# Cross attention on 64-row tiles: high and low parts of keys and queries placed under one another by DMA

## The chip, the cores and the metric

The kernel runs on one core of a Trainium2 chip. It is one program with one launch. The metric is the time of the whole execution on the device in microseconds (us); here that is the median of three runs. Below, PE is TensorE (PEld its weight loads), DVE is VectorE, ACT is ScalarE, POOL is GpSimd and SP is SyncE, which here only issues DMAs.

## The reference, cut to what matters

The input is x (32 batches, 112 tokens, 512 wide) and a memory of 375 rows of 256 for each batch. A first layer attends to the memory and gates the result. A second layer has causal self attention with two sets of weights (experts, chosen token by token by a mask), then the cross attention to the memory, then a gated MLP with two experts. The change is inside the cross attention:

```
cq = heads(rms_norm(hidden) @ cq_w, 16, 16)          # 112 x 256 -> 16 heads of 16
ck, cv = split(encoder_outputs @ ckv_w)              # 375 x 256 each, 16 heads of 16
scores = (cq / sqrt(16)) . ck                        # 16 heads, 112 x 375
p = softmax(scores)
hidden = hidden + (p . cv) @ cdense_w                # 256 -> 512
```

All is float32. The kernel reaches the accuracy with the matmul type float32r: a value is split into a high part (rounded to that type) and a low part (the rest), and a product a.b is taken as hi.hi + hi.lo + lo.hi.

## The kernel before, in words

The program runs six stages, a to f, one after another on every engine; each engine has its own written order and they meet through semaphores. Stage e is the cross attention. It goes over the 32 batches as a software pipeline in steps s: in step s TensorE computes the keys, values and turned queries of batch s+1, the scores by row of batch s, the scores by key of batch s-1, and the context and output product of batch s-2. The order is written out by hand in `e_pe` (lines 1694 to 1753), `e_act` (1555 to 1587), `e_dve` (1800 to 1827), `e_sp` (1504 to 1512) and `e_pool`.

One batch goes through these steps:

- `e_key_products` (line 1278): 12 matmuls of 128 x 128 x 376 leave the keys of two tiles of 128 channels (8 heads each) in PSUM banks 4 and 5; `queries_turn` (1590) transposes the queries beside them (columns 376 to 487); `values` (1597) fills banks 6 and 7.
- `keys_queries_high` (1529) on ScalarE copies the keys' high part, and twice the queries' with a mask per parity of the head, since 32 rows hold two heads of 16 channels; `keys_queries_low` (1778) on VectorE makes the low parts in three instructions.
- `scores(b, u)` (1611) is the pass by row: five units (`S_UNITS`), of 3, 3, 3, 3 and 4 heads, each head with three matmuls (hi.hi, hi.lo, lo.hi) of 32 rows, 112 weight columns and 376 moving columns into PSUM banks 0 to 3. After each unit VectorE reduces the maximum of each head (`maximum`, 1756), and the next unit waits for that since it uses the same banks.
- `maximum_parts` (1764), `maximum_turn` (1667) and `maximum_turned` (1773) split the negated maxima into high and low parts, transpose them on TensorE and spread them with a mask over four row groups.
- `scores_by_key(b, u)` (1628) is the pass by key: three units (`KEY_UNITS`) of 32 matmuls with 125 weight columns and 224 moving columns into banks 4 to 7: three products for each of four row groups, and a fourth that adds the negated maxima with ones as weights. `exponents` (1543) on ScalarE turns a unit of 1792 columns into probabilities; the next unit waits for it.
- `context` (1651), `raw`, `turn`, `norm`, `back` and `dense` make the context, divide it by its sum and multiply it with the output weights. `store` on GpSimd scatters the rows.

SP loads a batch's memory (`load_memory`, 376 KB) and its queries (`load_queries`, 112 KB); its queue is otherwise free in this stage. The helper `split_products` (lines 109 to 111) issues the three products of a split matmul, so keys, values and output products all show under these lines.

Of the kernel before, what the change touches and what calls it, by code (L numbers as in the profile page):

```python
# [13 lines left out]
P = 128  # L14
BATCHES, SEQ, DIM = 32, 112, 512
CTX, CDIM = 375, 256
NB = 4
# [37 lines left out]
S_UNITS, KEY_UNITS = 5, 3  # L55
# [58 lines left out]
def build_xattn(nc, x_t, mem_t, mem_n, mem_e, weights, e_weights, q_weights, w_gate_mem, w_mem, b_gate,  # L114
                norms, norm0_row, pos, rope_tables, identity_in, causal_in, head_masks, head_rows, mask_rows,
                slot_consts, before_in, rows, qk_rows, v_rows, ctx_rows, h_rows, cq_rows, cd_rows, out_rows):
    with ExitStack() as ctx:
# [39 lines left out]
        cmask, hmask, minus_half = sb("cmask", [P, 2]), sb("hmask", [P, QUADS]), sb("minus_half", [P, NB])  # L157
# [56 lines left out]
        def keep_busy(pe, bank, count):  # L214
            for _ in range(count):
# [36 lines left out]
                 (norm_w[:], norms), (norm0[:], norm0_row), (gate_b[:], b_gate), (cmask[:], head_masks),  # L252
                 (hmask[:], head_rows)]
# [784 lines left out]
        ones_r = rv(25536, (KC + 1,))  # L1038
# [239 lines left out]
        def e_key_products(pe, b):  # L1278
            pe.wait_ge(e_m_lo, b + 1)
            if b >= 3:  # L1280
                pe.wait_ge(e_exp, KEY_UNITS * (b - 2))
            hi, lo = e_m_parts[b % 2]
            for t in range(CT):
                for k in range(CT):
                    w = slice((t * CT + k) * P, (t * CT + k + 1) * P)
                    split_products(pe, ps[:, e_key_bank(b) + t, 0:CEVEN], e_w_hi[:, 0, w], e_w_lo[:, 0, w],
                                   hi[:, k, :], lo[:, k, :], k == 0, k == CT - 1)
# [191 lines left out]
        e_scattered = [Later(done, 8 * BATCHES) for done in c_scattered]  # L1479
        e_cq = [fv(17504 + 256 * i, (CDIM,), SEQ) for i in range(2)]  # L1480
        e_cv = [fv(4096 + 1536 * i, (NKC, HEADS, 2 * CHD), KC) for i in range(3)]
        e_pt = fv(8704, (KEY_UNITS, 4, 4 * SEQ), KC)
# [3 lines left out]
        e_k_parts = [both(8192 + 1504 * i, (CT, CEVEN)) for i in range(3)]  # L1486
        e_q_parts = [both(12704 + 896 * i, (QUADS, SEQ)) for i in range(3)]
        e_c_parts = both(15392, (CT, SEQ))
        e_max_tok = [rv(16288 + 128 * i, (4, 2 * HEADS), SEQ) for i in range(2)]
        e_max_t = rv(16544, (QUADS, SEQ))  # L1490
        key_units = [[(0, 0), (0, 1)], [(0, 2), (1, 2)], [(1, 0), (1, 1)]]
        s_heads = [range(3 * u, 3 * u + 3 if u < S_UNITS - 1 else HEADS) for u in range(S_UNITS)]

        def e_sp(sp):
# [4 lines left out]
            def load_queries(b):  # L1499
                if b >= 2:  # L1500
                    sp.wait_ge(e_k, b - 1)
                sp.dma_start(e_cq[b % 2], cq_rows[b * SEQ:(b + 1) * SEQ]).then_inc(e_cq_loaded[b % 2], 16)

            sp.wait_ge(*d_scattered.at(16 * BLOCKS))
            load_queries(0)
            load_queries(1)
            base = sp.value_load(base_f[0:1, 0:1], min_val=W_F, max_val=W_F + F_CHUNKS)
            for c in range(RING):
                ring_load(sp, M_F + c, chunk_at(base, c))
            for b in range(2, BATCHES):  # L1510
                load_memory(b)
                load_queries(b)
# [15 lines left out]
        def e_act(act):  # L1528
            def keys_queries_high(b):
                at = e_key_bank(b)  # L1530
                act.wait_ge(e_k, b + 1)
                act.copy(e_k_parts[b % 3][0], ps[:, at:at + CT, 0:CEVEN]).then_inc(e_kq_hi, 1)
                hi = e_q_parts[b % 3][0].rearrange("p (t x) s -> p t x s", t=CT)
                for x in range(2):
                    act.activation(hi[:, :, x, :], ps[:, at:at + CT, CEVEN:CEVEN + SEQ], ACT.Copy,
                                   scale=cmask[:, x:x + 1]).then_inc(e_kq_hi, 1)
# [6 lines left out]
            def exponents(b, u):  # L1543
                act.wait_ge(e_st, KEY_UNITS * b + u + 1)
                if b:
                    act.wait_ge(e_ctx, 2 * (b - 1) + (1 if u == 0 else 2))
                act.activation(e_pt[:, u], ps[0:KC, 4:8, 0:4 * SEQ], ACT.Exp).then_inc(e_exp, 1)  # L1547
# [6 lines left out]

            values(0)
            values(1)
            keys_queries_high(0)
            for s in range(BATCHES + 2):
                if s + 1 < BATCHES:
                    keys_queries_high(s + 1)  # L1560
# [660 lines left out]
```

## Time and profile before

| | us |
|---|---|
| median of 3 runs (lowest, highest) | 2340.03 (2339.19, 2341.38) |
| the profiled execution, its own time | 2341.35 |
| its span in the profile | 2339.5 |
| PE busy | 2202.4 (94%) |
| DVE busy | 1338.8 (57%) |
| ACT busy | 1071.1 (46%) |
| POOL busy | 881.5 (38%) |
| granted TensorE clock, mean | 0.982 |

A busy share is a mean over six stages with different limits. The line of the DMA engines' share over 40 equal slices of the span (58.5 us each) is `DMA  6343415556454446641111111102534344344331`: the nine digits of 1 and 0 in the middle include the cross attention, which runs from about 1040 to 1620 us. Busy time counts compute instructions; matmuls are pipelined, so instructions of one engine can overlap, and a busy TensorE is not TensorE at its peak.

### The profile page before, as it was taken

The numbers are of one execution on the slowest core, as the hardware profiler recorded it, in microseconds if no ns is written. First come the engines' busy times: TensorE is split into PE (matmuls) and PEld (weight loads), VectorE is DVE, ScalarE is ACT, GpSimd is POOL, SyncE is SP. The second block draws the span as 40 slices with busy tenths as digits, with TensorE's granted clock in tenths as the row PEclk, the third lists the DMA queues.
The fourth block names the chain that finished last, engine by engine and source line by source line (L and its number), as shares of the span: only waits on it lengthen the run. The fifth ranks groups of instructions, "written<-read, shape, count | busy, mean of one in ns | idle before, by whom it ended". The sixth has DMA issues, their size and how long they took to land.

```text
span 2339.5 us, 46940 instructions
## 1 busy us (share of the span) xinstructions
PE 2202.4 (94%) x19542; PEld 1835.6 (78%) x19542; DVE 1338.8 (57%) x1919; ACT 1071.1 (46%) x1842; POOL 881.5 (38%) x738
## 2 busy tenths in 40 slices
PE   7999999999799999988999999997999999999998
PEld 6899987778666668877777777775888888888887
DVE  6656537787589975546666666663534444434332
ACT  5343434333177755534555555553543344334332
POOL 2210127767434324521222111110745455555553
PEclk9999999999899999988999999998999999999999
DMA  6343415556454446641111111102534344344331
GB/s 227 129 161 112 173 52 209 201 199 222 157 175 139 138 131 247 235 159 35 42 40 50 42 40 50 42 22 106 179 124 160 113 133 136 128 133 122 104 113 45
DMA packets 107602, 293.88 MB, mean 126 GB/s; under 512 B 14560, under 2 KB 19008, under 8 KB 100736
## 3 DMA queue, kind: packets, MB, share of 16 engines
q1 hardware_dynamic: 88672, 230.60, 29.9%
q0 software_dynamic: 18720, 60.29, 7.0%
q8 instruction: 155, 2.54, 0.5%
q14 instruction: 55, 0.45, 0.1%
HBM read 221.65 MB, written 69.18 MB: 124 GB/s over the span
## 4 chain that ended last, share of the span: by engine, by line
PE 79%; DVE 8%; ACT 7%; DMA 2%; issue 2%; POOL 1%; SPq 0%; POOLq 0%; DVEq 0%; ACTq 0%
PE ps L109 19%; PE ps L111 18%; PE ps L110 18%; PE ps L1625 4%; PE ps L1662 4%; PE ps L1644 3%; DVE f_arena L995 3%; ACT f_arena L1547 2%; PE ps L1164 2%; PE ps L627 2%; ACT f_arena L1112 1%; DVE f_arena L991 1%; PE ps L1175 1%; DVE f_arena L987 1%; ACT f_arena L1118 1%
## 5 line engine op out<-in xcount | busy, mean ns | idle before, releaser
L109 PE MATMUL ps<-r_arena 128*128 128x512 f32 (+6 forms) x2410 | 902.7, 375 | 28.4 <-DVE r_arena L177 14.2
L177 POOL TENSOR_TENSOR r_arena<-f_arena,r_arena 128x512 fp32r<-128x512 f32 (+1 forms) x438 | 589.1, 1369 | 857.9 <-ACT r_arena L1268 433.6
L111 PE MATMUL ps<-r_arena 128*128 128x512 f32 (+6 forms) x2410 | 882.6, 366 | 0.0
L110 PE MATMUL ps<-r_arena 128*128 128x512 f32 (+6 forms) x2410 | 882.1, 366 | 0.0
L109 PEld LDWEIGHTS ps<-r_arena 128*128 128x128 f32 (+2 forms) x2410 | 454.1, 188 | 120.8 <-issue 26.3
L111 PEld LDWEIGHTS ps<-r_arena 128*128 128x128 f32 (+2 forms) x2410 | 454.5, 189 | 66.2
L110 PEld LDWEIGHTS ps<-r_arena 128*128 128x128 f32 (+2 forms) x2410 | 455.0, 189 | 60.0
L199 ACT CAST r_arena<-f_arena 128x512 fp32r<-128x512 f32 x400 | 235.6, 620 | 172.6 <-PE ps L111 135.4
L1761 DVE TENSOR_REDUCE e_negmax<-ps 112x3 f32<-112x1125 f32 (+1 forms) x160 | 225.2, 1408 | 104.2 <-PE ps L1625 101.5
L1547 ACT ACTIVATE f_arena<-ps 125x1792 f32<-125x1792 f32 x96 | 159.8, 1665 | 98.3 <-PE ps L1647 97.8
L2047 DVE SCALAR_TENSOR_TENSOR f_arena<-f_arena,ps 128x512 f32<-128x512 f32 (+1 forms) x88 | 57.4, 652 | 235.2 <-ACT f_arena L1937 235.2
L1941 ACT CAST r_arena<-f_arena 128x512 fp32r<-128x512 f32 (+1 forms) x88 | 52.2, 593 | 248.2 <-DVE f_arena L2051 248.2
L177 DVE TENSOR_TENSOR r_arena<-f_arena,r_arena 128x512 fp32r<-128x512 f32 (+4 forms) x141 | 113.2, 819 | 70.6 <-ACT r_arena L1941 58.1
L1644 PE MATMUL ps<-r_arena 32*125 32x224 f32 x2304 | 100.0, 284 | 39.9 <-ACT f_arena L1547 38.8
L1625 PE MATMUL ps<-r_arena 32*112 32x376 f32 x1536 | 123.1, 358 | 10.8 <-DVE e_negmax L1761 7.2
L1644 PEld LDWEIGHTS ps<-r_arena 32*125 32x125 f32 x2304 | 81.3, 184 | 66.0 <-ACT f_arena L1547 49.5
L2051 DVE SCALAR_TENSOR_TENSOR f_arena<-f_arena,ps 128x512 f32<-128x512 f32 (+1 forms) x88 | 57.6, 654 | 104.1 <-PE ps L111 103.8
L1937 ACT ACTIVATE f_arena<-ps 128x512 f32<-128x512 f32 (+1 forms) x88 | 50.2, 570 | 138.3 <-PE ps L111 138.3
L1625 PEld LDWEIGHTS ps<-r_arena 32*112 32x112 f32 x1536 | 74.5, 175 | 34.9 <-DVE e_negmax L1761 18.6
L177 DVE TENSOR_TENSOR r_arena<-ps,r_arena 128x224 fp32r<-128x224 f32 (+3 forms) x130 | 74.9, 591 | 39.8 <-ACT r_arena L528 15.7
L467 POOL TENSOR_TENSOR a_rstd<-a_ss,minus_half 112x2 f32<-112x2 f32 x16 | 11.3, 706 | 216.2 <-DVE a_ss L741 216.2
L995 DVE TENSOR_TENSOR f_arena<-f_arena 128x512 f32<-128x512 f32 x60 | 89.9, 1498 | 2.1
(201 smaller groups left out, 2738.3 us busy)
## 6 DMA issues: line engine op xcount, KB each, us to landing
f_arena<-weights SPq DMA_DIRECT2D x400, 256.0 KB, 3.0
f_arena<-rows SPq DMA_DIRECT2D x14, 1160.0 KB, 5.3
f_arena<-qk_rows SPq DMA_DIRECT2D x32, 448.0 KB, 3.9
f_arena<-mem_n SPq DMA_DIRECT2D x8, 1536.0 KB, 7.6
f_arena<-mem_e SPq DMA_DIRECT2D x32, 376.0 KB, 3.2
f_arena<-mem_t SPq DMA_DIRECT2D x16, 750.0 KB, 5.5
h_rows<-f_arena SPq DMA_DIRECT2D x7, 1160.0 KB, 4.8
f_arena<-h_rows SPq DMA_DIRECT2D x7, 1160.0 KB, 5.2
```

The costliest lines, as they stand in the source:

```text
L109: first = pe.matmul(out, w_hi, x_hi, start=start, stop=False)
L110: pe.matmul(out, w_hi, x_lo, start=False, stop=False)
L111: return first, pe.matmul(out, w_lo, x_hi, start=False, stop=stop)
L177: return engine.tensor_tensor(out, source, high.bitcast(F32), ALU.subtract)
L199: act.copy(w_hi[:, m % RING, :], w_raw[:, m % RING, :]).then_inc(w_hi_made, 1)
L995: dve.tensor_tensor(b_qk[:, j, which * DIM:(which + 1) * DIM].rearrange("p (h d) -> p h d", h=HEADS), by_cos, by_sin, ALU.add).then_inc(b_ ...
L1547: act.activation(e_pt[:, u], ps[0:KC, 4:8, 0:4 * SEQ], ACT.Exp).then_inc(e_exp, 1)
L1625: last = pe.matmul(ps[0:SEQ, h - s_heads[u][0], 0:CEVEN], q[r, h // 4, :], k[r, h // 8, :], start=n == 0, stop=n == 2)
L1644: pe.matmul(ps[0:KC, 4 + i, out], k[r, t, m], q[r, 2 * t:2 * t + 2, :], start=n == 0, stop=False)
L1662: last = pe.matmul(ps[32 * a:32 * a + 32, 3, batch(n)], e_cv[b % 3][:, c, 4 * n + a, :], e_pt[:, unit, 2 * half + a // 2, batch(at + a % 2 ...
L1761: dve.tensor_reduce(e_negmax[:, b % 2, heads[0]:heads[-1] + 1], ps[0:SEQ, 0:len(heads), 0:CTX], AX_X, ALU.max, negate=True).then_inc(e_max ...
L2051: dve.scalar_tensor_tensor(act_h[:, s, w], act_a[:, s, w], 0.5, ps[:, bank + 1, w], ALU.mult, ALU.mult).then_inc(f_glu_made, 1)
```

## The change

Keys and queries of a head are laid out with their parts under one another: in the keys, rows 0 to 15 hold the high part, 16 to 31 the low part, 32 to 47 the high part again, and 48 and 49 ones; in the queries, the high part, the high part, the low part, and the two parts of the negated maximum. One matmul over 48 rows is then hi.hi + lo.hi + hi.lo, one over 50 rows adds the maximum too. A head takes one half of the array (rows 0 to 49 or 64 to 113), a pair of heads lies side by side. The channels of the weights are permuted so that tile i holds the heads of parity i, with the channel as the slow and the pair as the fast index of the partition; a transfer of 128 partitions into 16 partitions of 8 rows each then puts a part where it belongs. `place_both` issues 12 such transfers a batch on the queue of SP, `place_maximum` two small ones. The score scale is applied as its square root to both sides. Scores by row have six units of 3, 3, 3, 3, 2 and 2 heads in banks 0 to 2; scores by key six units of eight matmuls (125 weight columns, 112 moving columns) that alternate between banks 4, 5 and 6, 7. The orders of all engines are rewritten, and `context` of a batch moves to the start of its last step.

```diff
-S_UNITS, KEY_UNITS = 5, 3
+S_UNITS, KEY_UNITS = 6, 6
+HALF, PAIRS = 64, HEADS // 2
+E_SCALE = float(CHD) ** -0.25
...
+        e_kq_parts = both(8192, (CT, CEVEN + SEQ))
+        e_keys = [rv(10144 + 3008 * i, (PAIRS, CEVEN)) for i in range(3)]
+        e_queries = [rv(19168 + 896 * i, (PAIRS, SEQ)) for i in range(3)]
...
+            def place(b, wide, into, row, source):
+                for i in range(CT):
+                    at = HALF * i + row
+                    sp.dma_start(into[b % 3][at:at + CHD].bitcast(F32), source[:, i, wide].bitcast(F32)).then_inc(
+                        e_placed[b % 2].sem, 16)
...
+            def place_both(b):
+                if b >= 3:
+                    sp.wait_ge(e_st, KEY_UNITS * (b - 2))
+                sp.wait_ge(e_kq_hi, e_split(b))
+                place_high(b, keys, e_keys, (0, 2 * CHD))
+                place_high(b, queries, e_queries, (0, CHD))
+                sp.wait_ge(e_kq_lo, e_split(b))
+                place(b, keys, e_keys, CHD, e_kq_parts[1])
+                place(b, queries, e_queries, 2 * CHD, e_kq_parts[1])
+
+            def place_maximum(b):
+                sp.wait_ge(e_mxt_made, b + 1)
+                for i in range(CT):
+                    at = HALF * i + K_ROWS
+                    sp.dma_start(e_queries[b % 3][at:at + 2].bitcast(F32), e_max_t[2 * PAIRS * i:2 * PAIRS * (i + 1)].bitcast(F32)).then_inc(
+                        e_max_placed.sem, 16)
...
+            for s in range(BATCHES + 1):
+                if s + 3 < BATCHES:
+                    load_memory(s + 3)
+                if s + 2 < BATCHES:
+                    load_queries(s + 2)
+                if s:
+                    place_maximum(s - 1)
+                if s + 1 < BATCHES:
+                    place_both(s + 1)
...
+            def high(b, wide):
+                if b:
+                    act.wait_ge(*e_placed[(b - 1) % 2].at(PLACES * ((b - 1) // 2 + 1)))
                 at = e_key_bank(b)
+                act.activation(e_kq_parts[0][:, :, wide], ps[:, at:at + CT, wide], ACT.Copy, scale=E_SCALE).then_inc(e_kq_hi, 1)
...
             def scores(b, u):
                 if u == 0:
-                    pe.wait_ge(e_kq_lo, 3 * (b + 1))
+                    pe.wait_ge(*e_placed[b % 2].at(PLACES * (b // 2 + 1)))
...
-                for n, (q, k) in enumerate(((q_hi, k_hi), (q_hi, k_lo), (q_lo, k_hi))):
-                    for h in s_heads[u]:
-                        r = slice(32 * (h % 4), 32 * (h % 4) + 32)
-                        last = pe.matmul(ps[0:SEQ, h - s_heads[u][0], 0:CEVEN], q[r, h // 4, :], k[r, h // 8, :], start=n == 0, stop=n == 2)
+                for h in s_heads[u]:
+                    r = slice(HALF * (h % 2), HALF * (h % 2) + K_ROWS)
+                    last = pe.matmul(ps[0:SEQ, h - s_heads[u][0], 0:CEVEN], e_queries[b % 3][r, h // 2, :],
+                                     e_keys[b % 3][r, h // 2, :], start=True, stop=True)
...
+                t, c = key_units[u]
+                m = slice(c * KC, (c + 1) * KC)
+                for n in range(PAIRS // 2):
+                    for i in range(2):
+                        r = slice(HALF * i, HALF * i + MAX_ROWS)
+                        last = pe.matmul(ps[0:KC, 4 + 2 * (u % 2) + i, batch(n)], e_keys[b % 3][r, PAIRS // 2 * t + n, m],
+                                         e_queries[b % 3][r, PAIRS // 2 * t + n, :], start=True, stop=True)
```

The new order of TensorE in a step: context 0 of batch s-2, unit 0 of the scores by row, context 1, unit 1, the turn of the maxima, key products and turned queries of batch s+1, the turn of the context, unit 2, values, then scores by key of batch s-1 (units 0 to 5) with units 3, 4 and 5 of the scores by row and the two output products between them.

## Rows read from the trace of the kernel before

**Rows 1.** Timeline of ScalarE: start us, us, engine, line, operation, shapes; the key copy.
```profile
1078.47 0.79 ACT L1532 CAST r_arena<-ps 128x752 fp32r<-128x752 f32 x1 [3.19 <-PE ps L1593]
...
1550.97 0.79 ACT L1532 CAST r_arena<-ps 128x752 fp32r<-128x752 f32 x1 [2.67 <-PE ps L1593]
...
1568.47 0.79 ACT L1532 CAST r_arena<-ps 128x752 fp32r<-128x752 f32 x1 [2.67 <-PE ps L1593]
```
**Rows 2.** Busy time of each engine in a stretch, clock, DMA share, GB/s: 28 steps.
```profile
1078.00:1568.00 490.00, 455.73 (x7982) 373.57 (x7981) 308.06 (x420) 261.67 (x316) 87.08 (x64) 1.00 0.14 42
```
**Rows 3.** Timeline of TensorE in one step; in brackets idle time and what ended it.
```profile
1306.65 1.12 PEld L1662 LDWEIGHTS ps<-f_arena 125*32 125x32 f32 x48 [0.25 <-issue]
...
1315.02 0.41 PEld L1644 LDWEIGHTS ps<-r_arena 32*125 32x125 f32 x12 [0.38 <-issue]
...
1315.89 0.46 PEld L1625 LDWEIGHTS ps<-r_arena 32*112 32x112 f32 x12
...
1317.93 0.59 PE L1644 MATMUL ps<-r_arena 32*125 32x224 f32 x12 [1.25 <-ACT f_arena L1547]
```
**Rows 4.** Timeline of TensorE: two key products, nine matmuls apart.
```profile
1303.68 0.33 PE L110 MATMUL ps<-r_arena 128*128 128x376 f32 x1
...
1305.23 0.33 PE L110 MATMUL ps<-r_arena 128*128 128x376 f32 x1
```
**Rows 5.** Groups by line and shape in one step: busy us, mean ns; weight loads.
```profile
L1662 PEld LDWEIGHTS ps<-f_arena 125*32 125x32 f32 x96 | 2.2, 110 | 0.5 <-issue 0.5
...
L110 PEld LDWEIGHTS ps<-r_arena 128*128 128x128 f32 x4 | 0.8, 188 | 0.0
```
**Rows 6.** Timeline of a unit of scores and of VectorE in the same step.
```profile
1305.95 0.77 PE L1625 MATMUL ps<-r_arena 32*112 32x376 f32 x9
1306.06 0.62 DVE L1775 TENSOR_TENSOR r_arena<-ps,hmask 128x448 fp32r<-128x448 f32 x1 [2.61 <-PE ps L1671]
...
1306.78 1.33 DVE L1761 TENSOR_REDUCE e_negmax<-ps 112x3 f32<-112x1125 f32 x1
...
1308.02 0.93 DVE L177 TENSOR_TENSOR r_arena<-ps,r_arena 128x752 fp32r<-128x752 f32 x1
...
1308.87 0.80 DVE L1784 SCALAR_TENSOR_TENSOR r_arena<-ps,cmask,r_arena 128x224 fp32r<-128x224 f32 x2
...
1316.73 1.72 DVE L1761 TENSOR_REDUCE e_negmax<-ps 112x4 f32<-112x1500 f32 x1 [1.14 <-PE ps L1625]
```
**Rows 7.** Timeline of ScalarE in the same step: key copy, a 224-column copy, an exponent.
```profile
1305.96 0.79 ACT L1532 CAST r_arena<-ps 128x752 fp32r<-128x752 f32 x1 [2.67 <-PE ps L1593]
...
1311.01 0.35 ACT L1571 CAST r_arena<-ps 128x224 fp32r<-128x224 f32 x1 [0.32 <-PE ps L1683]
...
1316.22 1.66 ACT L1547 ACTIVATE f_arena<-ps 125x1792 f32<-125x1792 f32 x1 [0.50 <-PE ps L1647]
```
**Rows 8.** The queries' load: issue on SP, us to landing, stretches; memory's load last.
```profile
1305.96 0.33 SPq L1502 DMA_DIRECT2D f_arena<-cq_rows  x1
...
f_arena<-cq_rows SPq DMA_DIRECT2D x1, 112.0 KB, 1.9
...
1306.50:1307.00 0.50, 0.50 (x22) 0.35 (x20) 0.41 (x2) 0.50 (x3) 0.00 (x0) 1.00 0.07 14
1307.00:1307.50 0.50, 0.50 (x32) 0.50 (x24) 0.50 (x1) 0.44 (x2) 0.00 (x0) 1.00 0.70 215
...
1318.90:1319.40 0.50, 0.50 (x17) 0.36 (x9) 0.04 (x1) 0.28 (x1) 0.00 (x0) 1.00 1.03 380
```
**Rows 9.** Timeline of TensorE at the stage's head, and a stretch with its clock.
```profile
1041.78 1.28 PE L1625 MATMUL ps<-r_arena 32*112 32x376 f32 x9 [3.25 <-DVE r_arena L1784]
...
1057.15 0.68 PE L109 MATMUL ps<-r_arena 128*128 128x376 f32 x1
...
1061.08 0.44 PE L1593 MATMUL ps<-ident,f_arena 112*128 112x112 f32 x2
...
1042.00:1046.00 4.00, 2.91 (x20) 1.58 (x20) 1.50 (x2) 1.47 (x3) 0.00 (x0) 0.50 1.02 371
```

More of the change, by code:

```diff
@@ L1698, in e_pe @@
             queries_turn(0)
-            scores(0, 0)
-            for s in range(BATCHES):
-                if s == 1:
-                    pe.wait_ge(e_v_act, 2)
-                    pe.wait_ge(e_v_dve, 2)
-                if 2 <= s + 1 < BATCHES:
+            for s in range(BATCHES + 2):
+                old, now, new = s >= 2, s < BATCHES, 2 <= s + 1 < BATCHES
+                by_key = 1 <= s <= BATCHES
+                if old:
+                    context(s - 2, 0)
+                if now:
+                    scores(s, 0)
+                if old:
+                    context(s - 2, 1)
+                if now:
+                    scores(s, 1)
+                if by_key:
+                    maximum_turn(s - 1)
+                if new:
                     e_key_products(pe, s + 1)
@@ L1707, in e_pe @@
                     queries_turn(s + 1)
-                if s:
-                    maximum_turn(s - 1)
-                scores(s, 1)
-                if s >= 2:
-                    context(s - 2, 1)
-                if 2 <= s + 1 < BATCHES:
+                if old:
+                    turn(s - 2)
+                if now:
+                    scores(s, 2)
+                if new:
                     values(s + 1, range(1))
-                if s >= 2:
-                    turn(s - 2)
-                if 2 <= s + 1 < BATCHES:
+                if old:
+                    back(s - 2)
@@ L1732, in e_pe @@
-                if s:
-                    scores_by_key(s - 1, 2)
-                if s + 1 < BATCHES:
-                    scores(s + 1, 0)
-                if s:
-                    context(s - 1, 0)
-            b = BATCHES - 1
-            maximum_turn(b)
-            scores_by_key(b, 0)
-            context(b - 1, 1)
-            turn(b - 1)
-            scores_by_key(b, 1)
-            back(b - 1)
-            scores_by_key(b, 2)
-            for k in range(CT):
-                dense(b - 1, k)
@@ L1748, in e_pe @@
-            for t in range(CT):
-                context(b, t)
-            turn(b)
-            back(b)
-            for k in range(CT):
-                dense(b, k)
+                if now:
+                    scores(s, 3)
+                if by_key:
+                    scores_by_key(s - 1, 1)
+                if old:
+                    dense(s - 2, 0)
+                if by_key:
+                    scores_by_key(s - 1, 2)
+                if now:
+                    scores(s, 4)
+                if by_key:
+                    scores_by_key(s - 1, 3)
@@ L1755, in e_dve @@
+                if old:
+                    dense(s - 2, 1)
+                if by_key:
+                    scores_by_key(s - 1, 4)
+                if now:
+                    scores(s, 5)
+                if by_key:
+                    scores_by_key(s - 1, 5)
         def e_dve(dve):
```

216 lines of the change are left out of this document (101 added, 115 removed).

## The prediction, on record before the result

> **What bounds the kernel now.** The change touches only the cross-attention stage, so I read that stage and not the page's averages. Its place is first found by its own instructions: two copies of keys on ScalarE, one batch apart, start 17.50 us apart, and the first and the last such copy of the steady stretch are 490.00 us apart, 28 batches [rows 1]. So a batch costs 17.50 us, and 32 of them are a quarter of the span. The stretches of busy time show what that step is made of: TensorE is busy 455.73 of 490 us, 16.3 us a batch, VectorE 11.0, ScalarE 9.3, the DMA engines 0.14 of their time at full clock [rows 2]. The timeline of TensorE inside one step then shows where the remaining 1.2 us go: one wait, of 1.25 us, for the exponent, because all eight head groups of a unit by key are read out of the same four PSUM banks [rows 3]. Everything else in the step is TensorE's own work. So less work on TensorE should pay nearly one for one here, until another loop closes behind it. The DMA queues have much room on average; whether they have it in the form in which this change asks for it is the question of the case.
>
> **Scores by row.** Before, 48 matmuls of 32 rows a batch, three or four at once: each unit of three heads takes three turns, five units 15 turns. The nearest turn of 376 columns is one of the key products: nine of them start within 1.55 us, 0.17 us each [rows 4], so 15 turns are 2.55 us. After, 16 matmuls, two at once (rows 0 and 64): the units of three heads take two turns, those of two heads one, 4 x 2 + 2 x 1 = 10 turns, 1.7 us. Saved: 0.85 us a batch. From below: if two 64-row matmuls don't run side by side, 16 turns, 0.17 us lost; from above all but one turn a unit hidden, 1.5 us saved.
>
> **Scores by key.** Before, 96 matmuls of 224 columns (72 and 24), a unit of 32 in 0.87 us [rows 3]. After 48 of 112 columns, six units of eight. Both number and width are halved, but each matmul has weights of its own. Loads of 128 columns take 188 ns and loads of 32 columns 110 ns [rows 5], 0.81 ns a column, so 125 columns cost about 0.10 us of pure loading; four row tiles loading side by side give 32 / 4 x 0.10 = 0.8 us, which is the unit's 0.87. The loads set its time, not the columns. After, eight loads on two row tiles are 4 x 0.10 = 0.42 us a unit, 2.5 us a batch, against 3 x 0.87 = 2.6. Saved: 0.1 us. The ends: 1.4 us saved if the columns alone counted (112 / 376 x 0.17 = 0.05 us a turn, 24 turns), 2.4 us lost if nothing ran side by side (48 x 0.10).
>
> **Order of TensorE.** The new order changes tile shape 12 times a batch instead of 10; such a change shows as 0.25 to 0.38 us of issue before a load [rows 3], so some 0.4 us more with the extra waits that split the units (nothing to 0.8). The exponent wait goes: units by key alternate between two pairs of banks. What is late next is unit 1 of the scores by row, which follows unit 0 with only half a context (0.65 us) between: it has to wait for the maximum. From the unit's start to the reduce's start are 0.83 us and the reduce takes 1.33 [rows 6], so some 0.7 us of wait. Step by TensorE alone: 16.2 of work - 0.85 - 0.1 + 0.4 + 0.7 = 16.35 us.
>
> **VectorE and ScalarE** stay under that. Reduces: 4 of 1.33 and 2 of 0.94 (1.72 for four heads and 1.33 for three are 0.39 a head [rows 6]) = 7.2 us against 7.0; low parts in one instruction of 976 columns, about 1.2 against 0.93 + 0.80 [rows 6]; the maxima's spread over four groups shrinks from 0.62 to about 0.25. Sum 10.4 against 11.0. ScalarE: six exponents of half the size, about 0.9 each by the 1.66 of the whole [rows 7], plus one copy of 0.98 instead of 0.79 + 0.79: again 9.3 us. Both have room in 16.35; behind a waiting exponent stand ScalarE's output copy and then the key copy, and the first has over 1 us of slack in the new order.
>
> **The placing.** This is the new part. For each batch the queue of SP issues 12 transfers inside the chip: six of keys (128 packets of 1504 B, 192.5 KB) and six of queries (128 packets of 448 B, 57 KB), 1.50 MB in all, each from 128 partitions into 16. The unit 0 of scores waits for all of them. Their chain is a loop over batches. From the start of unit 0 of batch s:
> - unit 0 to its reduce, one turn shorter than now: 0.66; the reduce 1.33: 1.99
> - unit 1: 0.35, then key products of the next batch, 12 x 0.17 = 2.0, turns of queries and a change of shape: 0.4; together 4.75
> - high parts on ScalarE: 752 columns take 0.79 and 224 take 0.35 [rows 7], so 976 take 0.98: 5.75
> - a transfer's fixed part: the load of 112 KB of queries lands 1.9 us after its issue while its bytes move in about 0.5 [rows 8]: 1.4, so 7.15
> - T, the time in which the 12 transfers move. The low parts are ready 1.3 us after the high ones, behind eight queued transfers, so they add nothing.
> The step is at least 7.15 + T. It stays under TensorE's 16.35 up to T = 9.2, and over today's 17.50 from T = 10.35.
>
> **What waits behind it.** Unit 0 of the scores carries the new wait, and all of TensorE's order stands behind it. On SP the low parts' wait stands ahead of the loads of memory three batches on and of queries two batches on, which have more than a batch to spare; they move behind the placing, 0.5 MB, while TensorE works. ScalarE's key copy also waits until the batch before is placed, which unit 0 has seen already. The two small transfers of the maxima (two partitions each) are issued after unit 1 and wanted after key products, a unit and the values, 5 us later: hidden in their 2 us; uncovered they would cost 2 us a batch.
>
> The trace has no transfer into 16 partitions, so T has ends only. From below: the engines need (0.07 + 0.70) x 0.5 x 16 = 6.2 us of engine time for the 112 packets of 1 KB [rows 8], 55 ns each; taken by bytes that is 81 ns for 1504 B and 24 ns for 448 B, eight each per engine and transfer, 6 x 8 x 0.105 = 5.0 us. SP's own issue, 12 x 0.33 = 4.0 us, hides in that. From above: the fastest half microsecond writes 128 partitions at 380 GB/s [rows 8], 3.0 GB/s a partition; if a partition takes no more, 16 take 47 GB/s and T is 31.6 us. Each engine would write into a single partition instead of eight. The ends are a factor of six apart and no row lies between; their geometric middle is 12.6. I take 13: all 16 engines work at one narrow place at a time, and the small packets of the queries can only add.
>
> The Trainium skill, SBUF — State Buffer, section Door 1: The DMA port swizzle, says that partitions 0 to 15 reach four of 16 ports and measured 104 GB/s, and that two transfers to different halves barely overlap. By it T is 1.50 MB / 104 GB/s = 14.4 us, an estimate, and the time some 45 us more than mine. The same skill, DMA: Bandwidth & Descriptors, section Bandwidth, has the fabric at 435 GB/s for traffic inside the chip, which would make T 3.4 us and the change a gain. No row here shows either.
>
> **The clock.** With the step set by the placing, TensorE stands still before each unit 0. Its work after the key products is about 10 us, T plus fixed part 14.4: a gap of some 4 us. The rows show a gap of 3.25 us, after which the granted clock is 0.50, 1.2 GHz, and 15 us later 12 key products still take 3.9 us (1057.15 to 1061.08) instead of 2.0 [rows 9]. In the loop that adds 2.0 us, at most 2.8 with the two units, or nothing if the clock holds. I take 2.0.
>
> **Sum.** 7.15 + 13 + 2.0 = 22.15 us a step, 4.65 more than 17.50. Batches 1 to 31 pay it: 31 x 4.65 = 144 us. The head of the stage waits for its first queries by two to three microseconds more, the last two steps have no placing and save about as much. Against the profiled execution (span 2339.5, time 2341.35, so 1.85 lie around the span) that is 2485; its time is 1.32 above the median of the runs, so 2484 on their scale. One microsecond of T is 31 us of time; the rest of the loop is known to about 1 us.
>
> **Rivals.**
> A. The placing is hidden, T under 9.2. For it: the DMA engines are idle 86% of the stage and the low end is 5.0 us. Against: that needs 163 GB/s or more into 16 partitions. Then TensorE sets the step at 16.35, 31 x 1.15 = 36 us are won: 2304. With both scores terms at their upper ends the step is 14.4 and the time 2244; with little won there it is 2340. This is the other side; it decides below T = 10.35, and between 9.2 and 10.35 the gain runs out to nothing.
> B. A partition takes no more than its 128th part: T = 31.6, step 40.75, 31 x 23.25 = 721 us more, 3061. Only the upper end speaks for it; one engine per partition is the reason against it, since eight partitions are now served by one engine in turn.
> C. The change doesn't do what it says: the pairs of 64-row matmuls don't overlap. For it: the trace has no 64-row tile. Against: 32-row tiles overlap four at once. TensorE then needs 16.2 + 0.17 + 2.4 + 0.4 + 0.7 = 19.9 us, 31 x 2.4 = 74 us more, 2414; where the placing is as slow as I think it would be hidden.
> D. T falls between 10.0 and 10.7: within 0.2%.
>
> **How the numbers follow.** Forecast (T between 10.7 and 17, own range 2370 to 2600) 0.58; A 0.30; B 0.04; C 0.04; D 0.04. Within 0.2%, 4.7 us, is what a measurement of this kernel can't tell from no change. Faster is A, 0.30; same is D, 0.04; slower 0.66. For eight in ten the range has to reach into A: from 2285, which leaves out under one in ten of the deepest gains, to 2600, which leaves out B and the slowest T.
>
> **What the profile after would show.** Right: a step near 22 us between key copies; TensorE idle before unit 0 of the scores with a DMA named as releaser, around 4 us each; the twelve placing transfers in one burst with the DMA share near 1 but the GB/s near 115, and landing times that grow along the burst; the clock at 0.50 in part of each step; exponents no longer waited for. The score terms show in the spacing within a unit of three (two turns instead of three) and in a unit by key of 0.42 us. Wrong: a burst of 1.5 MB over in 5 to 9 us; unit 0 released by TensorE's own order or a maximum; a step at or under 17 us. If the transfers into rows 0 and 64 overlap, T halves and A holds.

## The result, and the profile after

| | before | after |
|---|---|---|
| median of 4 runs each on one chip (lowest, highest), us | 2339.61 (2337.43, 2341.38) | 2514.60 (2511.25, 2519.52) |
| ratio, 95% interval | | 1.075 (1.0726 to 1.0774) |
| profiled execution, its span | 2339.5 | 2509.4 |
| granted clock, mean | 0.982 | 0.936 |

The change costs 7.5%. The forecast was 2484, inside a range of 2285 to 2600. Where the 170 us of the spans lie is told by the key copies on ScalarE, one a batch. The timeline of ScalarE after (start, duration, engine, line) has them at:

```profile
1057.94 0.99 ACT L1594 ACTIVATE r_arena<-ps 128x976 fp32r<-128x976 f32 x1 [8.52 <-PE ps L1652]
1089.23 0.98 ACT L1594 ACTIVATE r_arena<-ps 128x976 fp32r<-128x976 f32 x1 [16.70 <-PE ps L1652]
...
1357.24 0.99 ACT L1594 ACTIVATE r_arena<-ps 128x976 fp32r<-128x976 f32 x1 [1.99 <-PE ps L1652]
...
1738.35 0.98 ACT L1594 ACTIVATE r_arena<-ps 128x976 fp32r<-128x976 f32 x1 [3.64 <-PE ps L1652]
```

The first row is batch 1's copy, the last batch 31's. Batch 3's starts at 1111.12, so 28 steps take 627.23 us, 22.40 each, where [rows 1] have 17.50: 137 us more. Batch 3's copy already stands 32.7 us later than before: that is the stage's head. After batch 31's copy another 3 us are lost up to the next stage, and some 3 us come back behind it.

The stretches of busy time (busy us of TensorE, its loads, VectorE, ScalarE, GpSimd; granted clock, DMA share, GB/s) of the steady part, then a burst of placing, then the part behind the wait:

```profile
1100.00:1560.00 460.00, 353.84 (x4179) 290.97 (x4168) 205.73 (x283) 179.92 (x250) 67.17 (x49) 0.85 0.68 101
1360.00:1366.00 6.00, 6.00 (x67) 4.87 (x66) 3.85 (x6) 4.74 (x7) 0.00 (x0) 1.00 1.15 135
1372.80:1380.20 7.40, 7.40 (x71) 6.14 (x72) 2.84 (x3) 1.27 (x3) 1.83 (x1) 0.63 0.07 23
```

Against [rows 2] TensorE has fallen from 93% to 77% busy and the DMA share has risen from 0.14 to 0.68. In the burst all DMA engines are taken (a share over 1), yet they move 135 GB/s; memory's load shows 380 GB/s at 1.03 [rows 8]. A full DMA share says nothing of bytes. The last row has the clock at 0.63 on the mean.

The burst carries more than the placing. These are the stretch from the first issue to unit 0 and the eight microseconds behind it:

```profile
1357.50:1373.00 15.50, 10.18 (x136) 8.42 (x135) 7.30 (x11) 7.21 (x10) 0.94 (x1) 0.95 0.98 141
1373.00:1381.00 8.00, 8.00 (x76) 6.34 (x76) 3.18 (x5) 2.07 (x3) 1.83 (x1) 0.67 0.04 13
```

In the first 15.5 us x 141 GB/s = 2.19 MB move, 0.69 more than the twelve transfers' 1.50: the loads of memory and queries and the store of the output, which the prediction had put behind the placing, move almost whole before unit 0 starts.

What holds each step together is the chain of waits from one key copy to the next (start, duration, what):

```profile
1357.24 0.99 ACT r_arena L1594
...
1358.30 0.59 SPq L1519
...
1364.72 0.61 SPq L1519
...
1365.37 7.39 DMA r_arena<-r_arena
1372.76 0.04 issue
1372.80 0.96 PE ps L1681 x3
1373.77 2.40 PE ps L1711 x48
1376.16 0.90 PE ps L1681 x3
1377.06 0.38 PE ps L1720
...
1379.95 0.21 PE ps L1652 x2
...
1380.18 0.99 ACT r_arena L1594
```

Twelve issues on SP, the placing, unit 0 of the scores, half a context, unit 1, the turn of the maxima, key products, key copy again. This step is 1.06 + 14.46 + 7.42 = 22.94 us; steps of some 21.9 and 22.9 alternate. Nothing of TensorE's work on units 2 to 5, values, scores by key and output is in it. The timeline of TensorE shows the other side of the loop, the wait before unit 0:

```profile
1366.12 1.36 PE L1711 MATMUL ps<-f_arena 125*32 125x112 f32 x48
1372.80 0.96 PE L1681 MATMUL ps<-r_arena 48*112 48x376 f32 x3 [5.32 <-DMA r_arena<-r_arena]
1373.69 2.47 PE L1711 MATMUL ps<-f_arena 125*32 125x112 f32 x48
...
1380.51 0.59 PE L1681 MATMUL ps<-r_arena 48*112 48x376 f32 x3
```

Half a context takes 1.36 us ahead of the wait and 2.47 behind it, a unit of three heads 0.59 where the clock is full and 0.96 behind the wait: the granted clock is 0.50, 1.2 GHz, after the standstill and is back at 1.00 at 1378.5, in the middle of the key products.

Last, SP's queue (issue time, count), which [rows 8] showed at 0.33 us a load:

```profile
1356.27 1.36 SPq L1542 DMA_DIRECT2D r_arena<-r_arena  x2
1358.30 7.68 SPq L1519 DMA_DIRECT2D r_arena<-r_arena  x12
```

From one of the twelve issues to the next are 0.64 us, and the two of the maxima take 0.66 each, although they write two partitions.

### The profile page after: what moved, and what is told of

It reads as the page before. It is cut to its first block, busy times and chain, and to the rows that moved or that the text cites. A ratio compares the mean times of both kernels' runs of the same rounds, so it can differ in the third digit from the quotient of the medians.

```text
span 2509.4 us, 42305 instructions
## 1 busy us (share of the span) xinstructions
PE 2236.8 (89%) x16982; PEld 1866.3 (74%) x16982; DVE 1313.0 (52%) x1890; ACT 1058.1 (42%) x1875; POOL 881.6 (35%) x738
## 4 chain that ended last, share of the span: by engine, by line
PE 63%; DMA 11%; SPq 9%; DVE 7%; ACT 6%; issue 2%; POOL 1%; POOLq 0%; DVEq 0%; ACTq 0%
PE ps L111 16%; PE ps L112 16%; PE ps L113 16%; DMA r_arena<-r_arena 9%; SPq L1519 8%; PE ps L1711 3%; DVE f_arena L996 3%; PE ps L1681 2%; PE ps L1164 2%; PE ps L628 2%; ACT f_arena L1112 1%; ACT r_arena L1594 1%; DVE f_arena L992 1%; PE ps L1175 1%; DVE f_arena L988 1%
## 5 line engine op out<-in xcount | busy, mean ns | idle before, releaser
L1681 PE MATMUL ps<-r_arena 48*112 48x376 f32 x512 | 122.1, 462 | 181.2 <-DMA r_arena<-r_arena 172.2
L1681 PEld LDWEIGHTS ps<-r_arena 48*112 48x112 f32 x512 | 57.3, 211 | 207.8 <-DMA r_arena<-r_arena 180.3
L1606 ACT ACTIVATE f_arena<-ps 125x896 f32<-125x896 f32 x192 | 167.1, 923 | 39.6 <-PE ps L1699 39.6
L1699 PEld LDWEIGHTS ps<-r_arena 50*125 50x125 f32 x1536 | 112.2, 193 | 31.5 <-issue 21.9
L1578 POOL DMA_INDIRECT cd_rows<-f_arena,slot_all x32 | 29.9, 935 | 282.4 <-ACT f_arena L1644 282.4
L1612 ACT COPY f_arena<-ps 128x448 f32<-128x448 f32 x32 | 17.0, 533 | 262.3 <-PE ps L1711 262.3
L1699 PE MATMUL ps<-r_arena 50*125 50x112 f32 x1536 | 123.7, 276 | 2.2 <-DMA r_arena<-r_arena 2.2
L1711 PE MATMUL ps<-f_arena 125*32 125x112 f32 x3072 | 123.4, 330 | 0.0
L1711 PEld LDWEIGHTS ps<-f_arena 125*32 125x32 f32 x3072 | 103.5, 142 | 15.6 <-issue 13.5
```

The costliest lines, as they stand in the source:

```text
L1606: act.activation(e_pt[:, u], ps[0:KC, at:at + 2, 0:4 * SEQ], ACT.Exp).then_inc(e_exp, 1)
L1681: last = pe.matmul(ps[0:SEQ, h - s_heads[u][0], 0:CEVEN], e_queries[b % 3][r, h // 2, :], e_keys[b % 3][r, h // 2, :], start=True, stop=True)
L1699: last = pe.matmul(ps[0:KC, 4 + 2 * (u % 2) + i, batch(n)], e_keys[b % 3][r, PAIRS // 2 * t + n, m], e_queries[b % 3][r, PAIRS // 2 * t + ...
L1711: last = pe.matmul(ps[32 * a:32 * a + 32, 3, batch(n)], e_cv[b % 3][:, c, 4 * n + a, :], e_pt[:, NKC * t + c, a % 2, batch(2 * half + a // ...
```

## The experiments

Theory L, the prediction's: the step is a loop over batches through the placing, and T, the time in which the twelve transfers move, is set by how narrow the places are. The rivals: TensorE's own new work sets the step (P), the issues on SP set it (Q). Where the form or the number of the placings is edited, it is from batch 3 on. Each ratio is to the kernel before on the same chip, where its median was 2337 to 2347 us.

**Wider places.** Three kernels write the same bytes to other shapes of place: 128 partitions each, 32 with four pairs each, and 64 with two.

```diff
-                    sp.dma_start(into[b % 3][at:at + CHD].bitcast(F32), source[:, i, wide].bitcast(F32)).then_inc(
+                    n = row // CHD
+                    # e1_wide128:  to = into[b % 3][:, CT * n + i, :]
+                    # e2_wide32:   to = into[b % 3][HALF * i + 32 * (n // 2):HALF * i + 32 * (n // 2) + 32, 4 * (n % 2):4 * (n % 2) + 4, :]
+                    # e8_wide64:   to = into[b % 3][HALF * i:HALF * i + HALF, 2 * n:2 * n + 2, :]
+                    sp.dma_start(to.bitcast(F32), source[:, i, wide].bitcast(F32)).then_inc(
```

> From batch 3 on each of the 12 transfers of a batch writes the same 128 packets of the same size, but into 128 partitions of one pair's columns instead of 16 partitions of eight pairs (scores are then of other data, and the scale is a thousandth). Theory N, the narrow destination sets T: the burst of 1.5 MB moves at 300 GB/s or more, T falls from about 12 us to the pace of SP's issue (12 x 0.64 = 7.7 us) or below, the step falls to TensorE's own 16.3 to 17 us, time 2300 to 2340. Theory P, small packets inside the chip cost the same wherever they go: burst still near 125 GB/s, step near 22.4, time 2500 to 2520.

> As the run with 128 partitions, but each transfer goes into 32 partitions of four pairs (scores are of other data, scale a thousandth). Theory N with a limit that grows with the partitions reached: twice the rate, about 250 GB/s, T about 6 us, hidden behind SP's issue; step 16.5 to 17.5, time 2300 to 2350. If only one engine per partition mattered and not where they lie, the same. Theory P: 2500 to 2520.

> Each transfer into 64 partitions of two pairs from batch 3 on (other data, scale a thousandth). Measured so far in the burst: 125 GB/s into 16 partitions, about 140 into 32, over 300 into 128. Theory Q, successive packets of one DMA engine into one partition queue up and packets into different partitions overlap (an engine writes 8, 4, 2, 1 packets per partition at 16, 32, 64, 128): 64 lies clearly above 32, 180 to 250 GB/s, T near SP's issue of 7.7 us, time 2340 to 2390. Theory Ports of the Trainium skill (64 partitions reach no more ports than 32): burst as with 32 partitions, about 140 GB/s, time 2445 to 2465.

| written | time, us | ratio to before | mean step of 28, us |
|---|---|---|---|
| 128 partitions | 2334.1 | 0.9948 (0.9937 to 0.9960) | 16.5 |
| 64 partitions | 2440.8 | 1.0434 (1.0397 to 1.0471) | 19.9 |
| 32 partitions | 2455.3 | 1.0463 (1.0435 to 1.0491) | 20.4 |
| 16 partitions (the change) | 2514.6 | 1.075 (1.0726 to 1.0774) | 22.4 |

The stretches inside a burst, for 128, 32 and 64 partitions in turn:

```profile
1323.70:1324.70 1.00, 1.00 (x15) 0.86 (x13) 0.92 (x3) 0.41 (x1) 0.00 (x0) 1.00 0.93 325
```
```profile
1340.00:1345.00 5.00, 5.00 (x51) 3.87 (x51) 3.61 (x5) 3.76 (x5) 0.00 (x0) 1.00 1.11 133
```
```profile
1330.00:1335.00 5.00, 5.00 (x56) 3.87 (x55) 3.22 (x5) 3.76 (x6) 0.00 (x0) 1.00 1.16 141
```

With 128 partitions the bytes go at 325 GB/s and the change, otherwise whole, is a gain of 0.5%: the form of the placing costs the 7.5%, not its bytes, not its count of transfers. These 325 GB/s are the fastest microsecond; over its 8.7 us of issues this run moves 162 GB/s, the pace of the issues. 32 and 64 partitions take 2.0 and 2.5 us off the step, but inside the burst they gave 133 and 141 GB/s, no rate that grows with the partitions reached. Against the expectation of 250 for 32, and of 180 to 250 for 64 by theory Q of that run, "how narrow" is not the whole of it.

**Fewer transfers, and none.**

```diff
+                if b < 3:
                     place_high(b, queries, e_queries, (0, CHD))
...
+                if b < 3:
                     place(b, queries, e_queries, 2 * CHD, e_kq_parts[1])
```

> From batch 3 on the six transfers of queries are left out (the queries of batches 0 to 2 are used again): 77% of the bytes, half of the packets. Theory N by bytes: T falls from 12 to 9.3 us, step from 22.4 to 19.6, time about 2430. Theory P by packets: T halves to 6, the step falls to TensorE's 16.5 to 17.5, time 2300 to 2350.

> From batch 3 on nothing is placed (keys and queries of batches 0 to 2 are used again) and scores wait for the low parts alone. My theory: TensorE's own step is 16.35 us, the clock stays at 1.00, time 2304 (2290 to 2320), so the whole loss and more is the placing. Rival, the new order and the loads of the unit by key cost as much as they save: step 17.3 to 18, time 2335 to 2360.

Without the queries' transfers 2399.5 us (1.0225, 1.0198 to 1.0253), a step of 18.6: 3.8 less, of which the bytes are 2.8 (0.34 of 1.50 MB at 125 GB/s) and the rest probably a shorter cold part (the clock's mean from 1100 to 1560 us is 0.95, with the change 0.85). It fell between the two expectations, nearer that of the bytes. With no placing at all 2312.3 us (0.9853, 0.9832 to 0.9875). Its stretch over four steps:

```profile
1343.07:1405.47 62.40, 61.86 (x822) 50.98 (x821) 40.57 (x56) 34.86 (x49) 11.04 (x8) 1.00 0.16 49
```

TensorE is busy 61.86 of 62.40 us: this is P alone, 15.6 us a step against 17.50 before. The new scores do save time, 1.9 us a step against 1.15 predicted. P falls as the cause of the loss.

**The clock.** The wait is filled with 24 matmuls that nothing uses.

```diff
                 if old:
                     context(s - 2, 0)
+                if now and s:
+                    pe.wait_ge(e_maxed, S_UNITS * s)
+                    keep_busy(pe, 0, 24)
                 if now:
                     scores(s, 0)
```

> 24 matmuls whose result nobody reads stand before unit 0 of each batch but the first, so that TensorE has 4.5 us of work in the wait for the placing. My theory on the clock: it stays at 1.00, the stretch from unit 0 to the key copy falls from 7.4 to about 5 us, step 22.4 to about 20, time about 2440. Rival, the clock costs nothing because what is slow lies beside the maxima: time 2510 to 2520. If the matmuls reach past the wait: above.

2455.2 us (1.0496, 1.0466 to 1.0526). TensorE's timeline in one step:

```profile
1344.78 4.75 PE L218 MATMUL ps<-causal,ident_b 112*112 112x448 bf16 x24
1349.63 0.59 PE L1681 MATMUL ps<-r_arena 48*112 48x376 f32 x3
1350.15 1.36 PE L1711 MATMUL ps<-f_arena 125*32 125x112 f32 x48
```
The stretch over five steps:

```profile
1314.29:1416.60 102.31, 99.62 (x1147) 78.12 (x1146) 50.71 (x70) 43.64 (x60) 13.79 (x10) 1.00 0.75 111
```

The clock stays at 1.00, unit 0 is back at 0.59 us and the half context at 1.36; unit 0's weight loads still wait 0.5 us for the DMA, so the filler does not reach past the wait. The step over 28 batches is 20.42 us; the clock's term is 22.40 - 20.42 = 1.98 us. The rest of the wait stays: TensorE is now 97% busy and the kernel still 5% slower than before, because filler is not progress.

**Two queues.** If SP's issues or one queue's order limit the burst, half of the high parts' transfers on ScalarE's queue should shorten it.

```diff
-                place_high(b, keys, e_keys, (0, 2 * CHD))
-                place_high(b, queries, e_queries, (0, CHD))
+                place_high(b, keys, e_keys, (0,))
+                place_high(b, queries, e_queries, (0,))
...
+                    # on ScalarE, behind the key copy
+                            act.dma_start(into[b % 3][at:at + CHD].bitcast(F32), e_kq_parts[0][:, i, wide].bitcast(F32)).then_inc(
```

> Four of the eight high transfers of a batch (the second copies of keys and queries) are issued from ScalarE's queue right after its copy; they run beside SP's transfers. The second copy of the keys goes into partitions 32 to 47 and 96 to 111 while SP writes 0 to 15 and 64 to 79, by the page's table the same ports. Theory Q: the engines alternate between two partitions and the burst moves at 180 GB/s or more, T 8 us, step 18 to 19, time 2370 to 2400. Theory Ports: no gain for the keys, only the issue overlaps, which the engines' queue hid anyway; step 21.5 to 22.5, time 2490 to 2520.

2524.8 us (1.0793, 1.0762 to 1.0825), a step of 22.9, the burst's stretch at a share of 1.15 and 129 GB/s. Q falls for this kernel: the transfers' own time covers the issues'. The Trainium skill (DMA: Bandwidth & Descriptors, section Issuing engines are not separate DMA queues) says that issuing from several engines saves only the time of the issue; this run agrees, with no gain.

**The loop cut open.** Key products go ahead of unit 0, so that the copy and the placing of the next batch no longer wait for units 0 and 1.

```diff
                 if old:
                     context(s - 2, 0)
+                if new:
+                    e_key_products(pe, s + 1)
+                if s + 1 < BATCHES:
+                    queries_turn(s + 1)
+                if by_key:
+                    maximum_turn(s - 1)
                 if now:
                     scores(s, 0)
```

VectorE's and ScalarE's orders follow it.

> The key products, turned queries and turned maxima of step s move ahead of unit 0 of the scores; the key copy moves ahead of the context's copy, the low parts behind the first maximum. The placing of batch s+1 then starts one copy after batch s is placed instead of behind unit 0, unit 1 and the key products. My theory, the loop is what counts: it is then 0.98 + 1.4 + 12.3 = 14.7 us, under TensorE's 15.6 to 16.3, and the time 2300 to 2330 (before is 2347 on that chip). Rival, the DMA engines are the bound: 12.3 us of placing and 2.4 of loads and stores of which nothing overlaps, and a key copy late behind others on ScalarE: step 17 to 19, time 2340 to 2400.

2347.0 us (1.0033, 1.0018 to 1.0047), the step 17.1 us on the mean, mostly 16.66. The placing moves its bytes no faster (119 and 126 GB/s in two of its bursts); 5.3 us of every step are gone by order alone. Theory L holds in what it says of the loop, but the expectation's 2300 to 2330 us was missed: step and time lie in the rival's ranges. It is still above before because batch 3's key copy stands 22 us later than before's, and 0.4 us a step win back only 12 of them.

The rival's reason isn't what the trace shows, though. From 1200 to 1500 us no more than two of 18 key copies wait for a placing (4.3 us together) and unit 0 waits for one by 0.3 us once. What comes up in each of the 18 steps is unit 2 of the scores, behind the second maximum, since VectorE now makes the low parts (1.16 us) between the first two maxima:

```profile
1326.67 0.59 PE L1681 MATMUL ps<-r_arena 48*112 48x376 f32 x3 [1.14 <-DVE e_negmax L1803]
```

That is the difference of 16.66 to the 15.6 us with no placing. In every fourth step (18.2 us) the clock also falls to 0.50 behind this wait for some three microseconds.

In the next kernel several things change together: a second buffer of parts for odd batches, the low parts behind both first maxima on VectorE, the maxima's transfers on ScalarE's queue, and two chunks of values around unit 2.

```diff
-        e_kq_parts = both(8192, (CT, CEVEN + SEQ))
+        e_kq_parts = [both(8192, (CT, CEVEN + SEQ)), [
+            fv(19040 + CT * (CEVEN + SEQ) * i, (CT, CEVEN + SEQ)).bitcast(F32R) for i in range(2)]]
...
-                if b:
-                    act.wait_ge(*e_placed[(b - 1) % 2].at(PLACES * ((b - 1) // 2 + 1)))
+                if b >= 2:
+                    act.wait_ge(*e_placed[b % 2].at(PLACES * (b // 2)))
```

> The early key products, and the parts to be placed have two buffers, so that the key copy of a batch no longer waits for the placing of the one before; the maxima's two small transfers go out from ScalarE's queue; on VectorE the low parts stand behind both first maxima and the norm, on TensorE a third of the values stands ahead of unit 2. My theory: the placing (12.3 us plus 1.4) and the loads (2.2) fit side by side with the other work, the step is TensorE's own 15.6 to 16.0 us and the time 20 to 35 us under before. Rival, the placing fills the DMA engines so that the step stays at 16.5 or more because unit 0 waits for it in some steps: within 5 us of before.

2315.2 us, 0.9881 (0.9857 to 0.9904) of before: 1.2% faster than the kernel before, some 8% faster than the change. Five steps of it:

```profile
1319.54:1398.88 79.34, 77.99 (x1028) 63.39 (x1027) 50.24 (x70) 43.59 (x60) 13.79 (x11) 1.00 0.95 144
```

15.87 us a step, 0.27 above the step with no placing: hidden at last, with TensorE 98% busy. TensorE's matmuls no longer wait for the second maximum, which took 1.1 us a step, most of the 1.2 us won. That the second buffer was needed is not shown, since no run has the one edit without the others. The run also gives the placing's engine time, the share of all 16 DMA engines times the stretch: 0.95 x 15.87 = 15.1 us of all engines a step, less the loads' 0.14 x 17.50 = 2.45 [rows 2], is 12.6 us.

**What makes the transfer slow.** Three kernels separate the reading from the writing side. In the first the keys' transfers read 16 partitions and write 128; in the second they read 16 and write the same 16; in the third all transfers read 64 partitions and write the same 64, same bytes and same packets. The second isn't as clean: its rows are contiguous on both sides, and the keys go in packets of some 12 KB, eight times as large (18792 packets in 300 us where the first has 28400, both in 13 batches).

```diff
+                    # e11_narrow_read: what = e_keys[(b - 1) % 3][at:at + CHD], to = into[b % 3][:, CT * (row // CHD) + i, :]
+                    # e12_16_to_16:    what = e_keys[(b - 1) % 3][at:at + CHD], to as in the change
+                    # e13_64_to_64:    what = source[HALF * i:HALF * i + HALF, :, wide], to = into[b % 3][HALF * i:HALF * i + HALF, 2 * n:2 * n + 2, :]
```

> As the run that writes 128 partitions, but the six transfers of keys read 16 partitions of the keys of the batch before (eight rows each) instead of 128 (other data, scale a thousandth). If only the written side is narrow-limited: as there, ratio to before 0.99 to 1.00, bursts of 200 GB/s and more. If an engine that stays in one partition is slow on either side, or the ports limit reads as they do writes: near 125 GB/s again, step 20 to 22.5, ratio 1.04 to 1.075.

> From batch 3 on the six transfers of keys copy 16 partitions into the same 16 partitions of the next buffer (the keys of batch 2 are carried on), queries as before. So far: 128 into 16, 32 and 64 partitions all move near 135 GB/s, 128 into the same 128 over 300, 16 into 128 again slow. Theory Narrow (few partitions on either side are few ports): 110 to 135 GB/s, ratio to before 1.06 to 1.08. Theory Crossing (what costs is that a packet leaves another partition than it enters, so the engines get in each other's way; a copy that stays in its partitions is fast): bursts over 250 GB/s in the keys, ratio 1.00 to 1.03.

> From batch 3 on each transfer copies 64 partitions of both tiles into the same 64 partitions (other data, scale a thousandth); packets as before. Narrow by the ports of the Trainium skill's table (64 partitions reach half of them): near 200 GB/s, T 7.7, ratio 1.00 to 1.02. Crossing: fast, bound by SP's issue as with 128 partitions, ratio 0.99 to 1.00. If 135 GB/s again, neither: then only a transfer over all 128 partitions is fast, ratio 1.04.

| reads, writes (partitions) | ratio to before | GB/s in the burst | placing's engine time a step, us |
|---|---|---|---|
| 128, the same 128 | 0.9948 | 325 (1 us) | 4.5 |
| 64, the same 64 | 1.0073 (1.0049 to 1.0098) | 239 to 247 (1 and 2 us) | 6.0 |
| 128, 64 | 1.0434 | 141 (5 us) | 10.5 |
| 128, 32 | 1.0463 | 133 (5 us) | 11.0 |
| 128, 16 (the change) | 1.075 | 135 (6 us) | 12.8 |
| 16, 128 (keys) | 1.0764 (1.0731 to 1.0796) | 120 (10 us) | 8.2 |
| 16, the same 16 (keys, large packets) | 1.0807 (1.0747 to 1.0867) | 126 (8 us) | 9.9 |

Engine time is the DMA share from 1100 to 1560 us times the mean step, less 2.45 for the loads and stores. In brackets is the length of the stretch that was read.

The stretches of the third and of the first:

```profile
1329.70:1330.70 1.00, 1.00 (x15) 0.86 (x14) 0.93 (x3) 0.39 (x1) 0.00 (x0) 1.00 0.97 247
1330.70:1332.70 2.00, 2.00 (x22) 1.51 (x22) 1.61 (x2) 1.73 (x2) 0.00 (x0) 1.00 0.89 239
```
```profile
1335.00:1345.00 10.00, 7.97 (x120) 6.52 (x118) 5.54 (x9) 6.31 (x9) 0.93 (x1) 1.00 0.73 120
```

The clean pair is 64 to 64 against 128 to 64: the same packets into the same places, at 1.7 times the rate. So the narrow place alone isn't to blame; what differs is that the fast copy reads few partitions and stays in its own. All copies that leave their partitions with these packets lie at 120 to 141 GB/s, whether 16, 32 or 64 are written or 16 read; the two that stay lie at 239 to 325, and there the width counts. Whether crossing alone is slow, only 16 to 16 could tell: it stays in its partitions and the kernel is as slow as with the change, but its packets are others, and its rate swings between 12 and 265 GB/s from one microsecond to the next. So it speaks against "only the crossing" and doesn't settle it.

Where 16 partitions are read, the share stays under 1 (0.73 here), the engine time is 8.2 us instead of 12.8 and the twelve issues on SP stretch to 12.4 us instead of 7.7, yet the step is no shorter. So it isn't the engines' time alone that runs out; what else it is, no run tells. Why a transfer that reads 128 partitions moves hardly faster into 32 or 64 than into 16 is open too: no run tells the packets' order from which engine serves which partition.

## Why the prediction was right

The forecast of 2484 us is 31 under the median, inside its range. By its steps, with what the chain's step (22.94) and the mean (22.40) show:

- **What bounds it.** Right: a loop over batches, not TensorE's work. Shown twice, by taking the placing away (15.6) and by leaving it and moving the key products (17.1).
- **Scores.** TensorE's own step was put at 16.35 and is 15.6. Two turns a unit of three heads show as expected (0.59 us for the unit's three matmuls against 0.77 for nine in [rows 6]); loads of eight take 0.51 us, not 0.42. The wait for the maximum before unit 1 was put at 0.7 us because half a context was put at 0.65; it takes 1.36, and in the run with no placing TensorE stands 0.1 us behind it, its weight loads 0.4. That is most of the 0.75 between the two steps.
- **Placing.** T of 13 and 1.4 of fixed part make 14.4; the chain has 14.46 from the first issue to unit 0. The value was the geometric middle of ends a factor of six apart, and its nearness is luck in good part: at the burst's 135 GB/s the 1.50 MB are 11.1 us (in engine time 12.6 to 12.8, at a share of 1.15), and the 0.69 MB of loads and stores, which the text put behind the placing, move in the same stretch. How much they add to the wait, no run tells. The reason given for T, one narrow place at a time, is borne out in part only: places of 64 partitions moved at 141 GB/s. By the Trainium skill's rule (SBUF — State Buffer, section Door 1: The DMA port swizzle), 104 GB/s, it would have been 14.4, an estimate; the burst shows 135, and the measurement decides. That it would be the shape and not the bytes is right by the runs.
- **Issue on SP.** Put at 4.0 us for twelve, it is 7.7. It cost nothing, since T covers it (no gain from a second queue); with 128 partitions the issues, 8.7 us there, set the pace.
- **The loop outside the placing.** Unit 0 to the end of the turned queries: 4.75 + 2.0 for the clock predicted, 7.42 there. Clock's term 2.0 predicted, 1.98 by the filled wait, but not where it was put: the text had 1.9 of it in the key products, which take 2.5 us instead of 2.0. The most is in the half context between units 0 and 1, 2.47 us instead of 1.36, which the loop did not name, and 0.75 in the two units. That the sum is the same is luck.
- **The steady sum.** 4.65 a step predicted, 4.90 measured: over 28 steps 130 and 137.
- **The head, mis-sized.** Batches 1 to 3 at 4.65 each and two to three microseconds for the first queries were 16 us; it is 32.7. Of these 12 are unit 0 of batch 0, which starts at 1053.98 instead of 1041.78 [rows 9]: the first queries are turned, copied, placed, and only then used, in series and at 1.2 GHz at unit 0 (0.96 us). Another 9 are one step: SP issues the next stage's eight weight loads of 256 KB between the first two placings (4.05 us of issues), and TensorE stands still behind them, in its timeline:

```profile
1082.05 0.96 PE L1681 MATMUL ps<-r_arena 48*112 48x376 f32 x3 [15.90 <-DMA r_arena<-r_arena]
```

  That is a step of 31.3 us (1057.94 to 1089.23). The text named the loads of memory and queries in SP's queue, not these; that they are the cause is read from the order, no run moves them.
- **The tail** was to give two to three back and took three: its last steps run cold too (a unit by key takes 1.09 us there, 0.64 in the steady part).

Sum: 137 + 33 + 3 - 3 = 170 against 144 predicted. The mechanism held; of the 26 us between, 17 are the head, 7 the step, and the tail's sign makes up the rest but for 3 us that come back later. The other 4 to 5 us up to the median lie between the profiled executions and the medians.

Rival A, the hidden placing, needed T under 9.2 and had 0.30; it is excluded by T. B (31.6 us) and C (pairs that don't overlap) are excluded by T and by the 0.59. D's bounds were not worked out rightly: 0.35 us on either side of 10.35 are 11 us of time, not the 4.7 of 0.2%, and the clock's 2.0 us, which the forecast has in the loop, stand in neither bound. The forecast doesn't hang on them.

## What to carry to other kernels

Before a copy inside the chip is put between two matmuls, ask which loop it closes: here 14.5 us of latency cost 4.9 us a step while the next batch's key products stood behind the scores that wait for the copy. Moving the key products ahead of these scores won back 5.3 us a step by order alone, and 6.5 with the edits of the last kernel. Don't judge such a copy by its bytes: a busy share of 1.15 stood beside 135 GB/s. Its engine time (share times stretch) says what it takes from other transfers, but it is only a floor: with the narrow read it fell from 12.8 to 8.2 us and the step did not. A step that lengthens a pipeline is paid again at the stage's head, where nothing covers it.

## What the runs showed of the hardware

- Copies inside the chip that stayed in their partitions were fast, the wider the faster: 128 to the same 128 gave 325 GB/s, 64 to the same 64 gave 239 to 247. Copies that left them gave 120 to 141: from 128 into 16, 32 or 64, and from 16 into 128. 16 into the same 16, in packets of some 12 KB, gave 126 on the mean.
- Into 32 and 64 partitions the copies moved at 133 and 141 GB/s. The Trainium skill (SBUF — State Buffer, section Door 1: The DMA port swizzle) has 189 and 196 for 32 and 64 partitions. That 64 is worth hardly more than 32 agrees; the level doesn't, for copies inside the chip that change their shape, and here the measurement decides.
- SP's issue of a copy inside the chip took 0.64 to 0.66 us for 7 KB as for 188 KB, and up to 1.03 on the mean where 16 partitions were read (12.4 us for twelve). A load took 0.33 us before (112 and 376 KB alike, [rows 8]) and 0.43 to 0.59 in most steps of the change, behind the copies in the same queue.
